# One attention layer over edge steps: score pass, softmax and value pass joined into one pass, with sums kept in SBUF

## The reference, cut to what matters

```python
x = x + gcn(relu(layernorm(x)))            # layer 0, three sums over edges
h = relu(layernorm(x))
q, k, v = h @ Wq, h @ Wk, h @ Wv           # 4 heads of 8
scores = einsum('ehd,ehd->eh', q[dst], k[src]) / sqrt(8)
m = segment_max(scores, dst)
e = exp(scores - m[dst])
denom = segment_sum(e, dst)
msg = segment_sum(e[:, :, None] * v[src], dst)
x = x + (msg / max(denom, 1e-16)).reshape(N, 32) @ Wo
x = x + relational(relu(layernorm(x)))     # layer 2, by edge type
x = x + tensor_product(relu(layernorm(x))) # layer 3
```

## Time and profile before

| | |
|---|---|
| median of 3 runs | 14667.21 us |
| the profiled execution | 14664.15 us |
| its span, first to last instruction | 14662.5 us |
| PE busy | 6149.2 us (42%) |
| VectorE (DVE) busy | 6591.4 us (45%) |
| ScalarE (ACT) busy | 2546.6 us (17%) |
| GpSimd (POOL) busy | 9728.6 us (66%) |
| mean granted TensorE clock | 0.656 |
| HBM read / written | 657.66 MB / 158.81 MB |

### The profile page before, as it was taken

The page is one execution under the profiler, slowest core; times in us unless marked ns, Lnnn a source line. Parts: engine busy times, 40 slices in busy tenths (PEclk is TensorE's granted clock), DMA queues, the critical chain, the costliest instruction groups (busy, mean ns, idle before and its releaser), DMA issues. The chain is left out here.

```text
span 14662.5 us, 136870 instructions
## 1 busy us (share of the span) xinstructions
PE 6149.2 (42%) x28632; PEld 4084.8 (28%) x28633; DVE 6591.4 (45%) x14427; ACT 2546.6 (17%) x4127; POOL 9728.6 (66%) x10318
## 2 busy tenths in 40 slices
PE   3322222444443222222111112438888877555556
PEld 1111111233332111111000001323333346444445
DVE  5522222233332333443222226759999972333332
ACT  1122222455554111111000000000000011000001
POOL 0377777777776777774777773327777763777773
PEclk9655555677776555555555555559999995777776
DMA  3111111233322111113333332324444442111112
GB/s 99 24 29 29 29 29 29 72 80 80 80 79 55 23 23 23 23 23 107 79 78 79 78 79 53 86 53 82 83 83 82 82 93 61 24 23 23 24 23 52
DMA packets 749108, 826.80 MB, mean 56 GB/s; under 512 B 340806, under 2 KB 514225, under 8 KB 745878
## 3 DMA queue, kind: packets, MB, share of 16 engines
q0 software_dynamic: 340624, 383.65, 14.9%
q1 hardware_dynamic: 259246, 297.17, 7.1%
q10 hardware_dynamic: 148312, 136.41, 3.2%
HBM read 657.66 MB, written 158.81 MB: 56 GB/s over the span
## 5 line engine op out<-in xcount | busy, mean ns | idle before, releaser
L1180 POOL DMA_INDIRECT sum0g_ring<-scratch_parts,k_group_src x1568 | 1560.2, 995 | 836.1 <-issue 477.5
L718 POOL DMA_INDIRECT rel_ring<-scratch_tab,k_src x1664 | 1573.1, 945 | 609.9 <-issue 489.9
L718 POOL DMA_INDIRECT sh_ring<-scratch_tab,k_src x1664 | 1569.9, 943 | 559.0 <-issue 506.8
L718 POOL DMA_INDIRECT score_ring<-scratch_tab,k_src x1664 | 1577.9, 948 | 544.5 <-issue 506.8
L1180 POOL DMA_INDIRECT sum2g_ring<-scratch_parts,k_group_src x1568 | 1534.9, 979 | 523.4 <-issue 477.6
L1180 POOL DMA_INDIRECT sum1g_ring<-scratch_parts,k_group_src x1568 | 1538.2, 981 | 506.9 <-issue 477.4
L640 PE MATMUL rel_accumulator<-rel_message,rel_onehot 128*128 128x512 f32 x3328 | 1556.6, 611 | 399.6 <-DVE rel_message L2235 395.3
L640 PE MATMUL sh_accumulator<-sh_message,sh_onehot 128*128 128x248 f32 x3328 | 1199.1, 540 | 944.0 <-DVE sh_message L2461 940.2
L640 PEld LDWEIGHTS sh_accumulator<-sh_message,sh_onehot 128*128 128x128 f32 x3328 | 941.5, 290 | 1201.1 <-issue 1024.9
L1887 PE MATMUL score_q_edge<-query_parts,score_onehot_t 128*128 x1664 | 256.6, 259 | 1818.5 <-DVE score_onehot_t L604 1817.0
L1243 PE MATMUL sum0g_totals<-sum0g_rows,sum0g_onehot 128*128 128x98 bf16 x3136 | 295.4, 283 | 1659.4 <-ACT sum0g_rows L1229 1659.4
(11 more groups left out here) (421 smaller groups left out, 13492.9 us busy)
## 6 DMA issues: line engine op xcount, KB each, us to landing
rel_rel_rows<-scratch_rel_rows ACTq DMA_DIRECT2D x211, 256.0 KB
score_rows<-scratch_rel_rows SPq DMA_DIRECT2D x208, 256.0 KB, 3.7
scratch_kv<-score_ring SPq DMA_DIRECT2D x208, 256.0 KB, 2.0
value_ring<-scratch_kv SPq DMA_DIRECT2D x208, 256.0 KB, 2.6
rel_type_rows<-scratch_type_rows ACTq DMA_DIRECT2D x211, 172.0 KB
rel_ring<-scratch_tab,k_src POOLq DMA_INDIRECT x1672
score_ring<-scratch_tab,k_src POOLq DMA_INDIRECT x1664
sh_ring<-scratch_tab,k_src POOLq DMA_INDIRECT x1664, 2.4
```

The costliest lines, as they stand in the source:

```text
L718: nc.gpsimd.indirect_dma_start(out=ring[:, q, g, :], out_offset=None, in_=table, in_offset=bass.IndirectOffsetOnAxis(ap=k["src"][:, n * G ...
L1180: nc.gpsimd.indirect_dma_start(out=ring[:, n % slots, g, :], out_offset=None, in_=table, in_offset=bass.IndirectOffsetOnAxis(ap=k["group_s ...
```

## The change

The three stages become one, `attention_pass`. All engines walk through 236 iterations (208 groups and 28 more), written out without hardware loops.

- Score work of group n is as before, but its PSUM result has one pair of banks instead of three, each half released by its own product.
- A block of 128 steps is dealt with while later groups are scored: `scan_block` at iteration 4 of the next 16, `carry_block` (borders of the block, with a running maximum that is carried from block to block) at 6, `top_block` at 8 (the exponential follows on ScalarE), `weigh_block` at 10. Each needs a round trip through TensorE (`flip_block`, which runs one iteration earlier in TensorE's order).
- The maximum of a node that goes on in the next block can rise. So what was summed for it is multiplied by exp(old maximum - new maximum): `shrink`, spread over places by a small matmul and applied by `join_group` once per block.
- `make_parts` of group n - 27 (LAG = 27): the one-hot, weight copy, value product and three-part split, all on VectorE. SyncE reads the values back from `scratch_kv` three iterations ahead.
- TensorE adds each step of a group into one of eight places of a PSUM region of two banks, by the step's tile counted from the group's first tile (`slot_at`, made in `step_tables`). There are two such regions.
- `join_group` of group n - 28 on VectorE loads the tile number into a register, adds the three parts of all eight places in one reduction and adds the result to eight tiles of the sums in SBUF. ScalarE clears the region.
- `wo_join`, `wo_clear`, and `_take_tiles` go.

```diff
+                by_group = tile_row.rearrange("o (n g) -> o n g", g=G)
+                nc.vector.tensor_tensor(slot_row[:], by_group, by_group[:, :, 0:1].to_broadcast([1, GROUPS, G]), ALU.subtract).then_inc(numbered, 1)
+                dve.wait_ge(numbered, 3)
+                nc.vector.tensor_single_scalar(k["slot_at"][:], slot_row[:].rearrange("o n g -> o (n g)"), float(P), op=ALU.mult)
...
+SCAN_AT, CARRY_AT, TOP_AT, WEIGH_AT = 4, 6, 8, 10
+LAG = PER_BLOCK + WEIGH_AT + 1
...
-        q_edge = psum("q_edge", [P, 3, 2, BANK])
+        q_edge = psum("q_edge", [P, 2, BANK])
+        accumulator = psum("accumulator", [P, 2, 2 * BANK])
+        turned = psum("turned", [P, BANK])
...
+        def carry_block(dve, chain, b):
+            last_max, first_max = edge_rows[:, 0, :], edge_rows[:, 1, :]
+            coming, going = bounds[:, 0, :], bounds[:, 1, :]
+            chain.link(v.tensor_copy(last_dst[:, 0:1], last_dst[:, P:P + 1]))
+            chain.link(v.tensor_copy(ahead[:, 0:1], ahead[:, P:P + 1]))
+            dve.wait_ge(flipped, b * FLIPS + 2)
+            seen = turned[0:HEADS, :].rearrange("h (n e) -> h n e", n=4)
+            v.tensor_copy(edge_rows[:], seen[:, 0:2, :])
+            v.tensor_copy(first_dst[:], seen[:, 2, :])
+            chain.link(v.tensor_copy(last_dst[:, 1:P + 1], seen[:, 3, :]))
+            v.tensor_tensor(whole[:], first_dst[:], last_dst[:, 1:P + 1], ALU.is_equal)
+            chain.link(v.tensor_tensor(cont[:], first_dst[:], last_dst[:, 0:P], ALU.is_equal))
+            chain.link(v.tensor_tensor(limit[:], whole[:], cont[:], ALU.mult))
+            chain.link(limits(limit[:]))
+            chain.link(v.scalar_tensor_tensor(out=last_max[:, 0:1], in0=limit[:, 0:1], scalar=ahead[:, 0:1],
+                                              in1=last_max[:, 0:1], op0=ALU.min, op1=ALU.max))
+            chain.link(v.tensor_tensor_scan(ahead[:, 1:P + 1], limit[:], last_max, -BIG, ALU.min, ALU.max))
+            chain.link(v.memset(whole[:, P - 1:P], 0.0))
+            chain.link(v.tensor_tensor(whole[:, 0:P - 1], whole[:, 0:P - 1], cont[:, 1:P], ALU.mult))
+            chain.link(limits(whole[:]))
+            chain.link(v.tensor_tensor_scan(behind[:, ::-1], whole[:, ::-1], first_max[:, ::-1], -BIG, ALU.min, ALU.max))
+            chain.link(limits(cont[:]))
+            v.memset(going[:, P - 1:P], -BIG)
+            v.tensor_tensor(coming, ahead[:, 0:P], cont[:], ALU.min)
+            chain.link(v.tensor_tensor(going[:, 0:P - 1], behind[:, 1:P], cont[:, 1:P], ALU.min))
+            dve.sem_inc(read_back, 1)
+
+        def top_block(dve, chain, b):
+            dve.wait_ge(flipped, b * FLIPS + 3)
+            chain.link(v.tensor_copy(spread[:], turned[:, 0:2 * HEADS].rearrange("p (n h) -> p n h", n=2)))
+            for n, e in ((0, 0), (1, P - 1)):
+                chain.link(v.tensor_tensor(reset[:], dst[:, b, :], dst[:, b, e:e + 1].to_broadcast([P, P]), ALU.is_equal))
+                chain.link(limits(reset[:]))
+                for h in range(HEADS):
+                    last = v.scalar_tensor_tensor(out=tops[:, h, :], in0=reset[:], scalar=spread[:, n, h:h + 1],
+                                                  in1=tops[:, h, :], op0=ALU.min, op1=ALU.max)
+                chain.link(last)
+            v.tensor_tensor(fall[:], spread[0:1, 0, :], tops[0:1, :, 0], ALU.subtract)
+            v.tensor_scalar(first_place[:], k["iota"][0:1, :], k["drel"][0:1, b * P:b * P + 1], None, ALU.is_equal)
+            v.tensor_tensor(by_step[:], by_step[:], tops[:], ALU.subtract).then_inc(read_back, 1)
+
+        def weigh_block(dve, chain, b):
+            dve.wait_ge(flipped, b * FLIPS + 4)
+            chain.link(v.tensor_single_scalar(shrink[:], shrink[:], -1.0, op=ALU.add))
...
+            v.tensor_copy(weight[:, b % 2, :, :], turned4.rearrange("p h e -> p e h")).then_inc(read_back, 1)
+            dve.wait_ge(read_back, b * FLIPS + 4)
+
+        def make_parts(dve, chain, m):
+            dve.wait_ge(loaded[m % R], (m // R + 1) * DMA)
+            if m >= 3:
+                dve.wait_ge(added, (m - 2) * G)
+            v.tensor_tensor(onehot[m % 3][:], columns[:], places[:, m * G:(m + 1) * G].unsqueeze(1).to_broadcast([P, P, G]), ALU.is_equal)
+            part_weight = weight[:, m // PER_BLOCK % 2, m % PER_BLOCK * G:(m % PER_BLOCK + 1) * G, :]
+            v.tensor_copy(message[:, :, D:width], part_weight)
+            v.tensor_tensor(message[:, :, 0:D].rearrange("p g (h d) -> p g h d", d=DHEAD),
+                            kept[:, m % R, :, D:2 * D].rearrange("p g (h d) -> p g h d", d=DHEAD),
+                            part_weight.unsqueeze(3).to_broadcast([P, G, HEADS, DHEAD]), ALU.mult).then_inc(messaged, 1)
+            dve.wait_ge(messaged, m + 1)
+            high, middle, low = (parts[m % 3][:, :, c * width:(c + 1) * width] for c in range(3))
+            chain.link(v.tensor_copy(high, message[:]))
+            chain.link(v.tensor_tensor(rest[:], message[:], high, ALU.subtract))
+            chain.link(v.tensor_copy(middle, rest[:]))
+            v.tensor_tensor(low, rest[:], middle, ALU.subtract).then_inc(parted, 1)
+            dve.wait_ge(parted, m + 1)
+
+        def join_group(dve, chain, m):
+            tile = dve.value_load(k["tile_no"][0:1, m * G:m * G + 1], min_val=1, max_val=TILES) - 1
+            if m % PER_BLOCK == 0:
...
+            dve.wait_ge(added, (m + 1) * G)
+            v.tensor_reduce(joined[:], accumulator[:, m % 2, :].rearrange("p (s w) -> p s w", w=P)[:, :, 0:3 * width]
+                            .rearrange("p s (c f) -> p s f c", c=3), axis=AX_X, op=ALU.add).then_inc(joins, 1)
+            dve.wait_ge(joins, m + 1)
+            own = sums[:, bass.ds(tile, G), :]
+            chain.link(v.tensor_tensor(own, own, joined[:], ALU.add))
...
+            def _(dve):
+                for n in range(GROUPS + LAG + 1):
+                    if n + 2 < GROUPS:
+                        make_one_hot(dve, n + 2)
+                    if n < GROUPS:
+                        make_scores(dve, n)
...
+                    m = n - LAG
+                    if 0 <= m < GROUPS:
+                        make_parts(dve, chain, m)
+                    if 0 <= m - 1:
+                        join_group(dve, chain, m - 1)
...
+            def _(pe):
+                for i in range(GROUPS + LAG + 1):
+                    if i < GROUPS:
+                        tiles = _tiles_of(nc, k, i)
+                        pe.wait_ge(made, i + 1)
+                        for g in range(G):
+                            b, at = g // HALF_G, g % HALF_G * W
+                            if i and at == 0:
+                                pe.wait_ge(used, 2 * i - 1 + b)
...
+                    m = i - LAG - 1
+                    if 0 <= m:
+                        slots = _slots_of(nc, k, m)
+                        pe.wait_ge(cleared, m + 1)
+                        pe.wait_ge(parted, m + 1)
+                        for g in range(G):
+                            nc.tensor.matmul(accumulator[:, m % 2, bass.ds(slots[g], 3 * width)], onehot[m % 3][:, :, g], parts[m % 3][:, g, :],
+                                             start=False, stop=True, skip_group_check=True).then_inc(added, 1)
...
+                    m = n - LAG + 3
+                    if 0 <= m < GROUPS:
+                        sp.wait_ge(spilled[m % DEEP], (m // DEEP + 1) * DMA)
+                        if m >= R:
+                            sp.wait_ge(messaged, m - R + 1)
+                        sp.dma_start(kept[:, m % R, :, :].rearrange("p g f -> p (g f)"),
+                                     dram["kv"][:, m * G * 2 * D:(m + 1) * G * 2 * D]).then_inc(loaded[m % R], DMA)
...
```

More of the change, by code:

```diff
@@ new lines, in attention_pass @@
+        edge_rows = sb("edge_rows", [HEADS, 2, P])
+        first_dst = sb("first_dst", [HEADS, P])
+        last_dst = sb("last_dst", [HEADS, P + 1])
+        whole = sb("whole", [HEADS, P])
+        cont = sb("cont", [HEADS, P])
+        limit = sb("limit", [HEADS, P])
+        ahead = sb("ahead", [HEADS, P + 1])
+        behind = sb("behind", [HEADS, P])
+        bounds = sb("bounds", [HEADS, 2, P])
+        spread = sb("spread", [P, 2, HEADS])
+        raised = sb("raised", [P, HEADS, P])
+        fall = sb("fall", [1, HEADS])
@@ new lines, in attention_pass @@
+        shrink = sb("shrink", [1, HEADS])
+        shrink_of = sb("shrink_of", [1, width])
+        first_place = sb("first_place", [1, P])
+        weight = sb("weight", [P, 2, P, HEADS])
+        kept = sb("kept", [P, R, G, 2 * D])
+        message = sb("message", [P, G, width])
+        rest = sb("rest", [P, G, width])
+        parts = [sb(f"parts{h}", [P, G, 3 * width], BF16) for h in range(3)]
+        onehot = [sb(f"onehot{h}", [P, P, G], BF16) for h in range(3)]
+        columns = sb("columns", [P, P, G], BF16)
@@ new lines, in flip_block @@
+        def flip_block(pe, b, turn):
+            if b * FLIPS + turn:
```

(36 more changed lines are left out.)

376 lines of the change are left out of this document (106 added, 270 removed).

## The result

The changed kernel takes 14087.75 us (median of 4 runs, 14078.73 to 14090.71) against 14666.72 us before: a ratio of 0.9606, with a 95% interval of 0.9595 to 0.9618, 579 us less. The forecast was 14129 us. The profiled execution took 14090.71 us, with a span of 14088.7; that is 573.4 us less than the profiled one before (14664.15).

What follows compares the result with a forecast made beforehand. GpSimd's gathers bound the score pass. From 8921.9, plus 83 (delays), 7.5, 138.6, 19.8 and 0.98, the next stage starts at 9171.8, not 9712.6; with 3 for tables, 14126, and 3 for the median, 14129 us; range 14030 to 14300.

Steps and rivals of the forecast that it cites:

- The bound: Score pass: GpSimd's gathers keep setting the pace at 10.02 us per group, with VectorE's 8.75 us fitting beside them; chance 0.74.
- Rival 2: Merged pass: VectorE becomes the bound, its instructions slowed beside gathers, 11.47 us per group, 218 us more, 14347; chance 0.14.
- Rival 4: Merged pass: TensorE and VectorE take turns, VectorE waiting for TensorE, 13.5 us per group, 14770 us; chance 0.05.
- VectorE's load: Merged pass, per group: score work 2.56, make_parts 2.90, join_group 2.05 and block work 1.24, together 8.75 us.
- VectorE's share of 85%: Expected sign in the new profile: VectorE busy about 85% of the merged pass.
- The tail: After the last score group: 28 iterations without gathers at 4.95 us each, 138.6 us, and the last block's 19.8.
- The block work: VectorE's scan_block, carry_block, top_block, weigh_block and the join's scaling, once per 16 groups: 19.8 us, 1.24 per group.
- the last score iteration: Term between the use of the last gather's rows and the tail: 7.5 us.
- What VectorE does to the gathers: Merged pass: new VectorE instructions delay gathers by 0.40 us per group, 83 us in all; bounds 0 and 145 us.
- The rule: A gather waits for a VectorE instruction's end if it runs 0.12 us after the gather's start.
- rival 3: Merged pass: the same instructions meet the same gathers in each group, up to 1.65 us lost, 260 more, 14389; chance 0.07.
- The tables: step_tables: slot_at adds two instructions over 1,664 columns, at most 1.9 us each, taken as 3 us on the path.

## Why the prediction was right, and where it was not

**The bound: right.** GpSimd's gathers set the pass before and after; VectorE took in softmax, value work and joins and still waits 447 us for rows. Giving GpSimd the product back costs 185 us. Rival 2 did not come: VectorE waits for the gathers, and GpSimd for VectorE nowhere. Rival 4 did not come either: no wait of VectorE's products for TensorE stands among its waits. A slow form beside gathers, which rival 2 feared for every instruction, came in the median for the cast L1954 alone of the instructions of every group (0.49 instead of 0.31 us).

**VectorE's load: right in sum, by parts that cancel.** In the full stretch a group took 8.5 us of busy time and holes, against 8.75. The reduction took 1.06 (1.05), the additions 0.46, the one-hot 0.68 (0.73), the first cast 0.49 in the median (0.31), the register load 0.67 (0.54) and a gap of 0.15 before the addition that the sum did not have. `top_block`'s eight took 0.29 each, back to back, instead of 0.387. VectorE's share of 85% was too high as busy time: 75% in the full stretch, with the holes before the joins and additions 83%, and less in the first 27 groups, which have no value work.

**The tail: right in sum, again by parts that cancel.** 169.9 us against 169.2 from the last gather's start to the last sum. Its price per iteration (4.95 forecast, 5.16 found) was 0.21 short, 5.7 us in 27 iterations. The 28th has only a join and took 2.3 us, for the sum had counted `make_parts` 28 times where it runs 27 times: 2.6 too much. The block work took 18.1 us instead of 19.8, the last score iteration 7.1 instead of 7.5. The runs with LAG 24 and 20 show the price itself.

**What VectorE does to the gathers: right in kind, the size is the step that missed.** The term was 83 us, the gathers took 44.6 longer; the 38 us between make up the miss (36 us in the profiled execution, in which the other terms give 2 back; 41 in the medians). The term took an average: 0.10 us for the one-hot and a rate for the rest. Part by part it had 21 us for the one-hot, 42 for the short instructions, 12 for the block work and 8 from rounding up; the trace has 5, 30 and 15, and 2 for the one-hot of the targets (L609); of these 52 us, 7 stood in the score pass before. Two things were wrong in it. The rule lacked the condition that the instruction begins clearly before the gather: of the 25 gathers that come to their point with over 0.03 us of the one-hot to run, the 12 that began within 0.02 us of it go free. And the phase was averaged out. VectorE starts when a gather lands, so in 116 groups the same subtraction meets a gather's point 0.19 us before its own end. That is 22 us; the 11 long holds of `top_block` are 13, all others 16. With 0.29 us of shift it is 82 us in all, with 1.4 us of PSUM copies 74, with the same time in SBUF additions 91, with an overlapping pair 60, against 52 in the changed kernel. That was rival 3's mechanism, given 0.07 and a price of 260 us, which took the whole length of three instructions; the true hold is the rest of one. Mechanism of a rival, size of the forecast: the range held because both sizes were small. That the forecast came within 0.3% is in this part luck: a shift of the order by 0.29 us, which the prediction had no means to place, moves the held time from 52 to 82 us.

The Trainium skill (SBUF — State Buffer, "SBUF: two separate sides") says that VectorE shares a pair of SBUF ports with GpSimd, that a VectorE instruction with two SBUF inputs takes it against GpSimd work that reads SBUF, and that whichever starts first keeps it for the whole instruction. Which operands count and who began first come out as it says (192 of 192 held against 0 of 76, and none of 72 under the product with an input in PSUM). The same section infers that such a `tensor_tensor` leaves the writing of descriptors alone, since it takes only the read side; a gather would then not be slowed by it. Here it is: 116 times by the subtraction L1955, 178 times by the added SBUF additions. Nor does a gather that began first block the other for its whole length: L1887, which begins with it, takes 0.72 us instead of 0.69. The section did not give the size: a gather is held only if such an instruction began clearly before it and still runs 0.12 us after its start, so VectorE's 7.7 us of work in a group cost 0.25 us (52 / 208).

**The tables: 0.8 us instead of 3.** The two added instructions take 1.88 and 1.01 us; from the cast just before them (L514) to the first gather of the pass it is 109.0 us instead of 108.2. So most of them lies beside other work of `step_tables`. 3.7 us more stand behind the attention, where nothing was changed; the same holds for single runs of one kernel, whose spans before the pass differ by more (first gather between 6819.0 and 6849.9 in these profiles).

## What to carry to other kernels

A stage that does not need the bounding engine can move under one that this engine bounds, even if it then fills another engine to 83%; price the overlap by the pipeline's depth, iterations times the tail's own period (28 x 5.2 us here), for that is what comes back, and then shorten the depth. Where VectorE works from SBUF beside GpSimd's gathers, look at the timeline of one iteration, not at averages: find which instruction is already running when a gather starts and still runs 0.12 us later, and shift the order. Issue the register load for an address right behind a long instruction, ahead of the next wait, so that it runs beside it.

## What the runs showed of the hardware that was not expected

- VectorE's wait for a register load is 0.67 us, and none if it is issued under an instruction of 0.68 us.
- A gather is held by a VectorE instruction with two SBUF inputs that began at least 0.05 us before it and still runs 0.15 us after its start (192 of 192), and ends 0.82 us after the end of that instruction. One that begins with the gather or later does not hold it (0 of 76). Some holds are longer, through several instructions without a gap: 1.22 us through four, which went away with one wait. Their cause is open.
- Some instructions are slower beside gathers: the cast L1954 takes 0.49 us or a little more in 116 of 180 groups of the pass, and 0.31 in the others and in the tail. No run tests the cause.
- Letting two added instructions overlap (0.1 us less VectorE time per group) made the kernel 41 us faster than having the second wait, 0.2 us per group and more than the time itself. The trace has 31 of the 41 us in the gathers, as VectorE then met them otherwise.
